# Cross-attention with layer norm: context and x transposed by DMA, projections and score pieces placed in other steps

## The reference

```python
q = (x @ Wq.T + bq); k = (ctx @ Wk.T + bk); v = (ctx @ Wv.T + bv)      # split into 16 heads
att = softmax(q k^T / sqrt(32))                                       # per head, 224 x 750
out = x + (att v) @ Wo.T + bo
out = (out - mean) / sqrt(var + 1e-5) * gamma + beta
```

## Time and profile before

| what | us |
|---|---|
| median of 3 timed runs | 669.68 (668.54 to 672.08) |
| profiled execution, its own time | 673.01 |
| its span, first to last instruction | 670.3 |
| PE busy | 647.2 (97%) |
| DVE busy | 477.8 (71%) |
| POOL busy | 455.2 (68%) |
| ACT busy | 331.4 (49%) |

### The profile page before, as it was taken

The page is one execution under the profiler, slowest core; times in us unless marked ns, Lnnn a source line. Parts: engine busy times, 40 slices in busy tenths (PEclk is TensorE's granted clock), DMA queues, the critical chain, the costliest instruction groups (busy, mean ns, idle before and its releaser), DMA issues.

```text
span 670.3 us, 15116 instructions
## 1 busy us (share of the span) xinstructions
PE 647.2 (97%) x5441; PEld 448.9 (67%) x5441; DVE 477.8 (71%) x680; ACT 331.4 (49%) x657; POOL 455.2 (68%) x458
## 2 busy tenths in 40 slices
PE   8999999999999999999999999999999999999893
PEld 7757676766776666766767667776667767665452
DVE  4667767778767786777767786677867777667865
ACT  4514645554555554554455545455445544545460
POOL 9303765777957587675957779575877758678942
PEclk9999999999999999999999999999999999999787
DMA  9392412232232232332233322322323201331000
GB/s 289 124 236 71 113 42 73 60 85 74 57 97 71 62 86 75 88 74 84 56 80 88 88 72 58 96 68 66 88 77 90 57 3 35 84 87 32 28 30 28
DMA packets 39562, 53.08 MB, mean 79 GB/s; under 512 B 13436, under 2 KB 25736, under 8 KB 39496
## 3 DMA queue, kind: packets, MB, share of 16 engines
q1 hardware_dynamic: 39496, 52.16, 29.2%
HBM read 24.52 MB, written 3.67 MB: 42 GB/s over the span
## 4 chain that ended last, share of the span: by engine, by line
PE 87%; DVE 5%; POOL 3%; issue 2%; DMA 1%; ACT 1%; SPq 0%; DVEq 0%; POOLq 0%; ACTq 0%
PE ps_task L504 39%; PE ps_scores L515 11%; PE ps_task L555 11%; PE ps_scoresT L539 11%; PE ps_task L467 6%; PE ps_task L477 2%; PE ps_scores L504 2%; PE ps_task L581 2%; DVE top L777 2%; POOL pair_sums L886 2%; PE ps_task L481 1%; PE ps_scoresT L524 1%; DVE y L751 1%; DVE parts L739 1%; DMA ctx_in<-in_ctx 1%
## 5 line engine op out<-in xcount | busy, mean ns | idle before, releaser
L777 DVE TENSOR_REDUCE top<-ps_scores 112x1 f32<-112x750 f32 x256 | 235.7, 928 | 114.1 <-PE ps_scores L515 113.5
L886 POOL TENSOR_TENSOR pair_sums<-probsT 125x672 f32<-125x672 f32 x122 | 198.8, 1629 | 164.7 <-ACT probsT L678 159.4
L678 ACT ACTIVATE probsT<-ps_scoresT 125x448 f32<-125x448 f32 x384 | 188.5, 546 | 121.5 <-PE ps_scoresT L539 118.5
L515 PE MATMUL ps_scores<-stacks 96*112 96x512 f16 (+1 forms) x512 | 126.7, 329 | 5.3 <-DVE top L777 4.1
L504 PE MATMUL ps_task<-wvT,ctxT 128*125 128x512 f16 x564 | 129.9, 380 | 0.7 <-DVE ctxT L741 0.7
L504 PE MATMUL ps_task<-ctxT,wkT 128*128 128x375 f16 x708 | 122.7, 323 | 0.1
L539 PE MATMUL ps_scoresT<-stacks 100*125 100x224 f16 x768 | 116.5, 267 | 1.3 <-ACT probsT L678 0.2
L539 PEld LDWEIGHTS ps_scoresT<-stacks 100*125 100x125 f16 x768 | 83.5, 138 | 32.0 <-ACT probsT L678 12.4
L504 PEld LDWEIGHTS ps_task<-wvT,ctxT 128*125 128x125 f16 x564 | 74.6, 136 | 39.6 <-DVE ctxT L741 0.9
L504 PEld LDWEIGHTS ps_task<-ctxT,wkT 128*128 128x128 f16 x708 | 68.8, 97 | 37.4 <-DVE v L744 0.5
L891 POOL TENSOR_TENSOR head_sums<-pair_sums 125x224 f32<-125x224 f32 x122 | 84.2, 690 | 10.4
(11 more groups left out here) (94 smaller groups left out, 594.3 us busy)
## 6 DMA issues: line engine op xcount, KB each, us to landing
stacks<-parts SPq DMA_DIRECT2D x256, 60.9 KB, 2.0
ctx_in<-in_ctx SPq DMA_DIRECT2D x16, 672.0 KB
stacks<-parts SPq DMA_DIRECT2D x128, 46.9 KB, 2.0
x_in<-in_x SPq DMA_DIRECT2D x8, 448.0 KB, 3.6
resid<-in_x SPq DMA_DIRECT2D x8, 448.0 KB, 3.8
out_y<-y SPq DMA_DIRECT2D x16, 224.0 KB, 2.3
stacks<-parts SPq DMA_DIRECT2D x128, 14.0 KB, 1.8
ctx_in<-in_ctx SPq DMA_DIRECT2D x16, 78.0 KB
```

The lines of the kernel that those rows point to most:

```text
L515: last = nc.tensor.matmul(ps_scores[0:QP, s % RING, keys], stacks[0:STACK_ROWS, g, h, NK + QP * q:NK + QP * q + QP], stacks[0:STACK_ROWS, ...
L678: nc.scalar.activation(probsT[0:KP, g % 2, h, 2 * j:2 * j + 2, :].rearrange("p k q -> p (k q)"), ps_scoresT[0:KP, piece % 2, 0:2 * NQ], AC ...
L777: nc.vector.tensor_reduce(top[0:QP, g % 2, HG * q + h:HG * q + h + 1], ps_scores[0:QP, s % RING, 0:NK], AX.X, ALU.max).then_inc(top_ready, 1)
L886: nc.gpsimd.tensor_tensor(pair_sums[0:KP], probsT[0:KP, g % 2, h, 0:3, :], probsT[0:KP, g % 2, h, 3:6, :], ALU.add).then_inc(pair_sums_rea ...
```

## The change

Context and x are no longer transposed by PE in the rounds. Their tiles are now 128 tokens (five of 128 and one of 110; x 128 and 96). ACT casts a tile as it was loaded to float16 (`token_high`), DVE subtracts that and writes the low part (`token_low`), both into one of four slots of `token_parts`, and SP turns the slot, 128 tokens by 1024 float16 numbers or 256 KB, with one DMA transpose into `ctxT` or `xT` (`turn`). This stands in the visits' steps 1, 9 and 17 and in steps 3 and 11. The first three K and Q tasks that read them wait for the DMAs. A turn waits for its slot's low part and for the last reader of the old content of `ctxT` or `xT`. The prologue still transposes with PE. The context's load buffer holds three tiles in place of six, so the second half is loaded in the round that splits it. `attn` and `recip` are written over `attn_sums`. Seven of the projections stand in other steps, and eight steps beside the four visits' have no task (before: none). Pieces are dealt by a table: so many ahead of the task and so many behind it.

```diff
-    CTX_PARTS = (slice(0, 112), slice(112, KP))
+    CT = -(-NK // P)
+    CTX_TILES = [slice(P * i, min(P * i + P, NK)) for i in range(CT)]
+    X_TILES = [slice(P * i, min(P * i + P, NQ)) for i in range(2)]
+    ROW_BLOCK = 16
+    NK_PAD = -(-NK // ROW_BLOCK) * ROW_BLOCK
+    HALF_TILES = CT // 2
...
+    PIECES_IN = ((0, 0), (0, 0), (1, 0), (2, 0), (2, 0), (2, 1), (1, 0), (2, 1),
+                 (0, 0), (0, 0), (1, 0), (2, 1), (1, 0), (2, 0), (2, 0), (2, 1),
+                 (0, 0), (0, 0), (2, 0), (2, 1), (1, 0), (2, 0), (2, 1), (1, 0),
+                 (0, 0), (0, 0), (2, 0), (2, 0), (2, 0), (2, 1), (1, 0), (2, 0))
...
-    NEXT = {2: ("ctxT", 0), 6: ("ctxT", 1), 10: ("ctxT", 2), 12: ("xT", 0), 13: ("K", 0, 0), 14: ("ctxT", 3), 15: ("V", 0),
-            16: ("ctxT", 4), 19: ("K", 1, 0), 20: ("ctxT", 5), 22: ("V", 1), 23: ("xT", 1), 24: ("K", 0, 1), 26: ("Q", 0),
-            27: ("V", 2), 28: ("Q", 1), 29: ("K", 1, 1), 30: ("K", 2, 0), 31: ("K", 3, 0)}
+    NEXT = {13: ("K", 0, 0), 14: ("K", 1, 0), 15: ("V", 0), 19: ("K", 0, 1), 22: ("V", 1), 24: ("Q", 0), 26: ("V", 2),
+            27: ("Q", 1), 28: ("K", 1, 1), 29: ("K", 2, 0), 31: ("K", 3, 0)}
+    SPLIT = {1: (("ctxT", 0), ("ctxT", 1)), 3: (("ctxT", 2),), 9: (("ctxT", 3), ("ctxT", 4)), 11: (("ctxT", 5),),
+             17: (("xT", 0), ("xT", 1))}
+    SPLIT_ORDER = [t for s in sorted(SPLIT) for t in SPLIT[s]]
+    SPLIT_SLOTS = 4
+    FIRST_READERS = (("K", 0, 0), ("K", 0, 1), ("Q", 0))
+    LAST_READERS = {("ctxT", 2): ("V", 3), ("ctxT", 3): ("V", 4), ("ctxT", 4): ("V", 5), ("ctxT", 5): ("V", 5),
+                    ("xT", 0): ("Q", 3), ("xT", 1): ("Q", 3)}
...
-        if t not in NEXT.values() or t[0] not in "KQV":
-            return []
-        if t[0] == "V":
-            return [("ctxT", t[1])]
-        return [("xT", 0), ("xT", 1)] if t[0] == "Q" else [("ctxT", i) for i in range(3 * t[2], 3 * t[2] + 3)]
+        if t[0] == "Q":
+            return [("xT", 0), ("xT", 1)]
+        first, n = (KP * t[1], KP) if t[0] == "V" else (KH * t[2], KH)
+        return [("ctxT", i) for i in range(first // P, (first + n - 1) // P + 1)]
...
-        ctx_in = sb("ctx_in", [P, KT, D])
+        ctx_in = sb("ctx_in", [P, HALF_TILES, D])
         x_in = sb("x_in", [P, 2, D])
-        ctxT = sb("ctxT", [P, 2, DT, NK], F16)
+        token_parts = sb("token_parts", [P, SPLIT_SLOTS, 2, D], F16)
+        ctxT = sb("ctxT", [P, 2, DT, NK_PAD], F16)
...
-        recip = sb("recip", [P, NQ])
         attn_sums = sb("attn_sums", [P, 2, NQ])
-        attn = sb("attn", [P, NQ])
+        attn, recip = attn_sums[:, 0], attn_sums[:, 1]
...
-        def pieces_of(s):
-            i = s % UNIT
-            return (2 * i - 4, 2 * i - 3) if i >= 2 else ()
+        def pieces_of(b, s, behind):
+            table = EVEN if isinstance(b, int) and (b == B or b == LAST and s >= UNIT) else PIECES_IN
+            slot = s - s % UNIT
+            first = sum(sum(n) for n in table[slot:s]) + (table[s][0] if behind else 0)
+            return range(first, first + table[s][behind])
...
+            def turn(t):
+                sp.dma_start_transpose(tokens_turned(t),
+                                       token_parts[0:padded_rows(t), split_place(t)[1]].rearrange("p a d -> p (a d)")).then_inc(turned[t], DMA)
...
+                def turn_when_free(t):
+                    sp.wait_ge(task_ready, after(LAST_READERS[t]) if t in LAST_READERS else before)
+                    sp.sem_inc(split_seen, 1)
+                    wait_split(t)
+                    sp.sem_inc(split_seen, 1)
+                    turn(t)
...
+                if has_next(b):
+                    for i in range(2):
+                        turn_when_free(("ctxT", i))
+                    wait_split(("ctxT", 2))
+                    load_ctx(b + 1, 1)
...
+                    fill(2, ("K", 2, 1), ("Q", 2))
+                if has_next(b):
+                    for i in range(2, CT):
+                        turn_when_free(("ctxT", i))
+                    if more_loads:
+                        load_ctx(b + 2, 0)
+                if 0 in tasks:
+                    fill(3, ("K", 3, 1), ("Q", 3))
+                if has_next(b):
+                    for i in range(2):
+                        turn_when_free(("xT", i))
+                    if more_loads:
+                        load_x(b + 2)
+                    fill(0, ("K", 0, 0), ("K", 0, 1), ("Q", 0))
...
-                        pe.wait_ge(task_saved, before + max([saved_by(b, s - TASK_BANKS) if not (isinstance(b, int) and b == B) else 0] + [tasks[STEP_OF[i]][1] + 1 for i in inputs_of(t)]))
+                        pe.wait_ge(task_saved, before + (saved_by(b, s - TASK_BANKS) if not (isinstance(b, int) and b == B) else 0))
+                        if t in FIRST_READERS:
+                            for i in inputs_of(t):
+                                pe.wait_ge(turned[i], DMA * batch_of(t, s, b))
...
+                    u = unit_before(b, g, 1)
+                    if u is not None:
+                        for piece in pieces_of(b, s, True):
+                            scores_keymajor(u, (g - 1) % UNITS, piece)
...
+            def token_high(t, batch):
+                if t[0] == "ctxT":
+                    act.wait_ge(ctx_loaded[t[1] // HALF_TILES], DMA * (1 + t[1] // HALF_TILES) * (batch + 1))
+                else:
+                    act.wait_ge(x_loaded, DMA * len(X_TILES) * (batch + 1))
+                held, back = slot_before(t)
+                need(act, turned[held], DMA * (batch - back))
+                rows_in = slice(0, padded_rows(t))
+                nc.scalar.copy(token_parts[rows_in, split_place(t)[1], 0], tokens_in(t, batch)[rows_in]).then_inc(token_high_saved, 1)
...
-                need(act, attn_scaled, u)
+                need(act, attn_low_saved, u)
...
+                    if has_next(b):
+                        for t in SPLIT.get(s, ()):
+                            token_high(t, b + 1)
...
+            def token_low(t, batch):
+                dve.wait_ge(token_high_saved, len(SPLIT_ORDER) * (batch - 1) + split_place(t)[0] + 1)
+                rows_in, slot = slice(0, padded_rows(t)), split_place(t)[1]
+                nc.vector.tensor_tensor(token_parts[rows_in, slot, 1], tokens_in(t, batch)[rows_in], token_parts[rows_in, slot, 0],
+                                        ALU.subtract).then_inc(token_low_saved, 1)
...
```

More of the change, by code:

```diff
@@ L63, in build @@
     EARLY_V = [t[1] for t in NEXT.values() if t[0] == "V"]
-    assert OWN.keys() | NEXT.keys() | OUTPUT.keys() == {s for s in range(STEPS) if s % UNIT != VISIT} and UNIT % TASK_BANKS == 0
+    assert all(s % UNIT != VISIT for t in (OWN, NEXT, OUTPUT) for s in t) and UNIT % TASK_BANKS == 0
     assert not OWN.keys() & NEXT.keys() and not (OWN.keys() | NEXT.keys()) & OUTPUT.keys()
@@ L350, in load_ctx @@
             def load_ctx(b, half):
[L351 to L354, removed]
-            def load_x(b):
-                sp.dma_start(x_in[0:QP], dram(x, b).rearrange("(q p) d -> p q d", p=QP)).then_inc(x_loaded, DMA)
+                tokens, home = dram(ctx_tokens, b), ctx_home(b, half)
+                whole = [i for i in range(HALF_TILES * half, HALF_TILES * half + HALF_TILES) if rows_of(("ctxT", i)) == P]
+                sp.dma_start(home[:, 0:len(whole)],
+                             tokens[P * whole[0]:P * whole[-1] + P].rearrange("(k p) d -> p k d", p=P)).then_inc(ctx_loaded[half], DMA)
+                if len(whole) < HALF_TILES:
+                    last = CTX_TILES[-1]
+                    sp.dma_start(home[0:last.stop - last.start, HALF_TILES - 1], tokens[last]).then_inc(ctx_loaded[half], DMA)
+            def load_x(b):
+                for i, rows_of_x in enumerate(X_TILES):
+                    sp.dma_start(x_in[0:rows_of(("xT", i)), i], dram(x, b)[rows_of_x]).then_inc(x_loaded, DMA)
+            def turn(t):
+                sp.dma_start_transpose(tokens_turned(t),
+                                       token_parts[0:padded_rows(t), split_place(t)[1]].rearrange("p a d -> p (a d)")).then_inc(turned[t], DMA)
             def load_resid(b):
@@ L395, in _ @@
             fill_stack(0)
-            for half in range(2):
-                load_ctx(1, half)
+            load_ctx(1, 0)
             load_x(1)
@@ L411, in after, with wait_split @@
                     return before + max(tasks[STEP_OF[t]][1] for t in kinds) + 1
-                def load_ctx_half(half):
-                    sp.wait_ge(task_ready, after(*[("ctxT", KT // 2 * half + i) for i in range(KT // 2)]))
-                    load_ctx(b + 2, half)
+                def wait_split(t):
+                    sp.wait_ge(token_low_saved, len(SPLIT_ORDER) * b + split_place(t)[0] + 1)
+                def turn_when_free(t):
[4 more added lines that the diff above has]
+                    turn(t)
                 def store_half(q):
@@ L473, in task @@
                 kind = t[0]
-                if kind == "ctxT":
```

(18 more changed lines are left out.)

76 lines of the change are left out of this document (43 added, 33 removed).

## The result

The changed kernel takes 683.6 us (median; 682.84 to 684.34) against 670.88 us for the kernel before beside it (668.54 to 673.1), a ratio of 1.0184, 95% interval 1.0154 to 1.0215: slower by 1.8%, where 658 was forecast. The profiled execution has a span of 681.0 us against 670.3. Its own time is 682.84 us against 673.01: what lies around the span is 1.8 us here and 2.7 there, so it is not the same in every execution, as I had written (1.8 to 2.9 us in the timed runs of the kernel before).

The account below looks back on a forecast made before the run. PE's stream of matmuls was taken to bound each round. Transposes removed, 3.36 us, less 1.7 of new waits gave 1.65 us a round, 11.6 over seven rounds: 669.7 - 11.6 = 658 us, range 646 to 690.

Parts of the forecast that it names:

- Mechanism of the turns: On SP's queue: a DMA transpose of one slot takes 2.3 us, so SP has 62 of 76 us a round.
- the sum's condition: SP and DVE have room: eight turns fit beside SP's 44 us a round if each holds its queue under 4.0 us.
- The rival with SP as the bound: Rounds last 44 + 8T once a turn holds SP for T of 4.0 us or more: slower, 687 to 945; chance 0.27.
- the 5.1 us by pieces: SP rival's turn time from 1024 pieces of 256 bytes at 79 ns each over 16: 84.8 us a round, 721 us.
- the estimate of 10.5 us by blocks: A turn as eight 128x128 blocks of 1309 ns one after another: 128 us a round, some 1020 us in all.
- the rival's 9.1 us and 945: Dear end of the SP rival, a turn as slow as the 224 KB broadcast row: 116.8 us a round, 945 us.
- No reader waits: At 2.3 us a turn, SP's turns land before the K and Q tasks that read them, so PE never waits.
- the deadline of tile 2: Its turn stands behind unit 2's stacks, which end at 22 us into a round; K in step 13 reads at about 28.5.
- This is the most it can bring on PE: Six context and two x transpose tasks leave PE's stream: 3.4 us in each of seven rounds, 23.5 us in all.
- ScalarE's waits: PE waits for exponentials at pieces, notably steps 21 and 31: 1.7 us a round given back, total waits from 12 to some 25 us.
- DVE's price: DVE's subtraction from SBUF taken at 0.67 us, 1.56 at the dear end; hidden at 0.67, some 0.5 us a round at 1.56.
- Four more waits of 0.49 us: Rival that the gain is eaten: DVE at its dear end, waits like the second O's, 2 us a round, 669 us; chance 0.12.

Follow-up runs that it names:

- the last version: Changed kernel with tile 2 turned first, x's splits in step 18, unit 1 dealt anew, units 2 and 3 two pieces a step, second reciprocal root later: 665.15 us.
- the run with two additions: Changed kernel without the third addition of each head's sum on GpSimd: 668.93 us, ratio 0.9952 to the kernel before.
- the four edits: Changed kernel with tile 2 turned first, all two-tile splits one step later, units 1 and 2 dealt anew, second reciprocal root with centering later: 677.57 us.

## Why the prediction was wrong

- **Mechanism of the turns: right, and the sum's condition held.** A turn holds SP for 1.26 us (median; 1.4 to 1.8 from one to the next), far from the 4.0 that would have made SP the bound. It lands after 3.3 us, later than the 2.3 that I took and the 2 to 3 that I named as the sign of being right. The rival with SP as the bound forecast the sign for a reason that did not occur; neither the 5.1 us by pieces nor the estimate of 10.5 us by blocks came. (That estimate gave 128 us a round and some 1020 us in all, so it is not the same as the rival's 9.1 us and 945, as I wrote.)
- **"No reader waits": wrong in one place.** I counted the deadline of tile 2 with a round of visits. The first round has none in its steps 1 and 9 and is some 5.6 us shorter there (2.8 a visit), while the stacks are not: SP issues them from 52.46 to 63.69, 11.2 us in place of 10.3. The price was not the wait alone but the clock behind it: 6.0 us by the run without turns, 2.3 of them in slow matmuls.
- **"This is the most it can bring on PE", 3.4 us a round: mis-sized.** The time from start to start of a transpose task was read as its price. It lay in a wait for exponentials which nothing reported, because PE was busy in it. Under the old order 2.5 us of it bring 0.4. With GpSimd nearly out of the way the whole change brings 1.0 us a round, where 1.65 was forecast. Which part of it turns the transposes' time into gain is not shown: in units 2 and 3 two pieces a step did as well or better (76.4 us a round in the last version).
- **ScalarE's waits: right in place and about in size.** 0.49 us idle at steps 21 and 31, waits of PE's loads for exponentials 25.2 us as against 25 forecast. Together the PE and ScalarE terms gave 76.0 us a round; 76.5 was measured with GpSimd's third addition left out.
- **The step that failed: what is late next.** I weighed DVE, ACT and SP and left POOL out of the working, though it was busy for 56.8 us of the round. Its head sums end on time by little in the old kernel. POOL's timeline there, the last head of unit 2 ahead of the visit of step 25:

```profile
323.06 1.61 POOL L886 TENSOR_TENSOR pair_sums<-probsT 125x672 f32<-125x672 f32 x1
324.74 0.73 POOL L891 TENSOR_TENSOR head_sums<-pair_sums 125x224 f32<-125x224 f32 x1
325.55 0.66 POOL L894 TENSOR_TENSOR head_sums<-head_sums,pair_sums 125x224 f32<-125x224 f32 x1
```

  The last addition ends at 326.21, and PE's sums of that visit, the first to read it, start at 326.49: 0.28 us to spare, and no wait to be seen; at step 17 it was 0.63 us (304.89 and 305.52), at step 1 2.5 us. In the changed kernel PE comes sooner (21.3 us from the visit of step 17 to that of 25, 19.9 without the 1.45 us lost in the first, against 21.0 before), and, under the new dealing, the exponentials of the last head before step 17 later; the sums are then late by 1.27 and 0.74 us. This is 1.9 us a round by the run with two additions, 13 us in seven rounds. With 6.0 us of the first round and 5 of the smaller gain (7 x 0.7) it makes up the distance of 24 us between the forecast 11.6 us less and the measured 12.7 us more.
- **DVE's price: between the bounds, and paid elsewhere.** A mean of 1100 ns in place of my 0.67 us where POOL adds at the same time, 743 ns with the splits moved. It did not bound PE by itself there; it made POOL's last sum 0.7 us longer at step 17.
- **A wrong sum among the rivals.** Four more waits of 0.49 us are 2.0 us a round, and 658.1 + 7 x 2.0 = 672, not 669.

Not settled: what PE's one gap of 2.09 us is, and how much of what the four edits lose is ScalarE's and how much VectorE's.

## What to carry to other kernels

Work taken from the busiest engine pays only as far as no wait stands behind it: shorten it in place first (one transpose for four), and read what takes its time. Before an engine is made to arrive earlier, list for each of its waits how long ago the other side was done; here the slack at two visits was under a microsecond, and the engine that had it did not appear among the waits. A schedule that is right in the steady rounds must be checked once more in the first, and an idle stretch can be paid twice, as here, by the wait (3.6 us) and by the clock (2.3 us).

## What the runs showed of the hardware

VectorE's subtraction of two SBUF tiles of 128x512 took 0.68 us at the least and 1.78 at the most, with a mean of 1100 ns in the changed kernel and 743 ns with the splits moved one step away from the visits; GpSimd's addition of 125x224 took 1.03 us beside it and 0.67 alone. The DMA transposes of 256 KB in SBUF held SP for 1.26 us (median) and landed after 2.8 to 4.9 us; they shared the queue with the stacks' DMAs, and no round but the first was longer for them. After 3.6 us without a matmul the granted clock was at 0.50 for the next 3.7 us (1.2 GHz), and at 1.00 in the rows from 72.31 on.
